# The last chunk of an expert layer finished as two half chunks, in two PSUM banks and with two stores

## The reference, cut to what matters

```python
g = jnp.einsum('th,ehi->tei', x, w1)            # 16 experts, inner width 64
u = jnp.einsum('th,ehi->tei', x, w3)
act = jax.nn.silu(g) * u
expert_out = jnp.einsum('tei,eih->teh', act, w2)
out = jnp.einsum('teh,te->th', expert_out, scores)   # scores: 4 of 16 experts are non-zero
...
x = _layernorm(x + out)        # (x - mean) / sqrt(var + 1e-5), over the 128 features of a token
```

## Time and profile before

| what | value |
| --- | --- |
| median of 3 runs | 384.11 us |
| lowest, highest run | 382.1, 384.95 us |
| the profiled execution's own time | 384.47 us |
| its span, as the trace shows it | 382.7 us |
| mean granted TensorE clock in it | 0.958 of full speed |
| TensorE, VectorE, ScalarE, GpSimd busy | 89%, 71%, 58%, 57% of the span |

### The profile page before, as it was taken

One profiled execution on the slowest core, in us unless ns is written; L12 is line 12 of the kernel. 1 busy time (PEld: TensorE's weight loads), 2 busy tenths in 40 slices (PEclk: granted clock), 3 DMA queues, 4 the chain that ended last, 5 costly groups with the idle time before them and its releaser, 6 DMA issues.

```text
span 382.7 us, 11549 instructions
## 1 busy us (share of the span) xinstructions
PE 339.9 (89%) x3556; PEld 264.8 (69%) x3556; DVE 270.0 (71%) x1247; ACT 222.7 (58%) x527; POOL 217.4 (57%) x405
## 2 busy tenths in 40 slices
PE   2876899999998998987889899999989999999992
PEld 1764687877777786875768688888755766565661
DVE  5733899999999989986647567777956259444444
ACT  1446488888999986867587566765553342222120
POOL 8667354688888887687873234330115355454551
PEclk9989589999999999999699899999999999999997
DMA  6989958888888898714654746565016410533411
GB/s 127 228 207 216 195 139 208 217 184 205 184 184 172 204 212 197 136 38 98 150 133 103 150 107 144 125 149 103 2 61 200 135 55 0 131 124 120 130 27 27
DMA packets 76927, 52.89 MB, mean 138 GB/s; under 512 B 34448, under 2 KB 68064, under 8 KB 76880
## 3 DMA queue, kind: packets, MB, share of 16 engines
q1 hardware_dynamic: 75840, 51.73, 57.1%
q0 software_dynamic: 512, 0.48, 1.0%
q10 hardware_dynamic: 528, 0.10, 0.1%
HBM read 32.24 MB, written 20.05 MB: 137 GB/s over the span
## 4 chain that ended last, share of the span: by engine, by line
issue 27%; PE 27%; POOL 23%; DVE 10%; ACT 5%; DMA 4%; SPq 2%; POOLq 1%; ACTq 0%; DVEq 0%
PE bank L1047 4%; PE bank L1051 4%; POOL rest L484 4%; POOL parts L490 4%; PE bank L1060 4%; POOL rstd L531 3%; DMA stk<-parts_dram 3%; PE bank L923 3%; PE bank L680 2%; PE bank L730 1%; POOL mixc L511 1%; SPq L361 1%; POOL gained L538 1%; PE bank L787 1%; DVE bank L1480 1%
## 5 line engine op out<-in xcount | busy, mean ns | idle before, releaser
L1480 DVE CUSTOM_DVE_ANT_0 bank<-bank,decayed_e 128x128 f32<-128x128 f32 x256 | 67.0, 323 | 1.0 <-issue 0.5
L649 POOL TENSOR_TENSOR stk<-stk 128x512 f32<-128x512 f32 x32 | 40.6, 1270 | 38.5 <-ACT stk L1354 35.8
L1491 DVE TENSOR_REDUCE top<-bank 128x4 bf16<-128x512 f32 x64 | 43.9, 687 | 22.4 <-PE bank L741 22.0
L1158 ACT ACTIVATE prob_t<-bank 128x512 f32<-128x512 f32 x64 | 38.7, 605 | 31.6 <-PE bank L770 31.1
L484 POOL TENSOR_TENSOR rest<-pf,parts 128x512 f32<-128x512 f32 (+1 forms) x32 | 29.2, 914 | 38.0 <-ACT parts L1137 37.7
L1354 ACT ACTIVATE stk<-bank 128x512 f32<-128x512 f32 x32 | 19.1, 597 | 53.6 <-PE bank L1047 53.6
L1148 ACT ACTIVATE prob<-bank 128x512 f32<-128x512 f32 x64 | 39.2, 613 | 18.2 <-PE bank L720 17.6
L1734 DVE TENSOR_TENSOR stk<-bank,stk 128x512 f32<-128x512 f32 x32 | 22.0, 691 | 39.1 <-POOL stk L649 38.0
L787 PE MATMUL bank<-prob_t,vmix 128*32 128x128 f32 x1024 | 43.0, 281 | 5.9 <-ACT pvs L1182 5.9
L490 POOL TENSOR_TENSOR parts<-rest,parts 128x512 bf16<-128x512 f32 (+1 forms) x32 | 29.3, 915 | 28.9 <-ACT parts L1141 28.7
L1468 DVE TENSOR_TENSOR decayed_e<-bank,decay 128x512 f32<-128x512 f32 x64 | 43.8, 685 | 0.5 <-issue 0.3
(11 more groups left out here) (201 smaller groups left out, 801.4 us busy)
## 6 DMA issues: line engine op xcount, KB each, us to landing
stk<-parts_dram SPq DMA_DIRECT2D x32, 384.0 KB, 5.3
stk<-shares_dram SPq DMA_DIRECT2D x64, 128.0 KB, 3.1
parts_dram<-parts SPq DMA_DIRECT2D x32, 192.0 KB, 2.4
parts_dram<-parts SPq DMA_DIRECT2D x48, 128.0 KB, 2.6
stk<-parts_dram SPq DMA_DIRECT2D x32, 192.0 KB, 3.7
parts_dram<-parts SPq DMA_DIRECT2D x32, 96.0 KB, 2.0
parts_dram<-parts SPq DMA_DIRECT2D x48, 64.0 KB, 1.8
w<-in_L_ffn_w_dram SPq DMA_DIRECT2D x3, 512.0 KB, 9.3
```

What stands on the lines that cost most here:

```text
L649: pool.tensor_tensor(h1[kk % 2], sg[kk % 2], share[kk], ALU.mult).then_inc(weighted, 1)
L1480: m = dve.tensor_tensor_reduce(out=bank[g % 2][:, 128 * j:128 * j + 128], in0=bank[g % 2][:, 128 * j:128 * j + 128], in1=decayed_e[:, g % ...
L1491: dve.tensor_reduce(top[:, b.par, GH * g:GH * g + GH], bank[S2_BANK[g % 2]][:].rearrange("p (h t) -> p h t", h=GH), AX.X, ALU.max).then_in ...
```

## The change

Chunks 0 to 2 are as before. In chunk 3 the down products of token blocks 0 and 1 go to bank 5 and those of blocks 2 and 3 to bank 7, in the same order of matmuls; of the last step each pair counts a semaphore of its own. The end of chunk 3 is made of four functions on VectorE, each for one half (two blocks), called in the order sum 0, statistics 0, sum 1, mean 0, statistics 1, mean 1, rows 0, rows 1. GpSimd makes one root of two columns for each half, and SyncE one store of 128 KB for each half. Seven semaphore names, eight semaphores in all, are new. The diff, with only the declarations cut:

```diff
...
@@ sync @@
-            store(NCH - 1)
-            sp.wait_ge(stored, 16 * NCH)
+            for m in range(2):
+                at = 4 * (NCH - 1) + 2 * m
+                sp.wait_ge(half_out[m], 2)
+                sp.dma_start(out[at:at + 2].rearrange("b t d -> t b d"), fout[:, 2 * m:2 * m + 2, :]).then_inc(stored, 16)
+            sp.wait_ge(stored, 16 * (NCH + 1))
@@ gpsimd @@
-            final_root(NCH - 1)
+            for m in range(2):
+                pool.wait_ge(half_eps, m + 1)
+                pool.tensor_tensor(frstd[:, 2 * m:2 * m + 2], fveps[:, 2 * m:2 * m + 2], minus_half[:, 0:2], ALU.pow
+                                   ).then_inc(half_root, 1)
@@ tensor @@
+            def down_halves(kk):
+
+                u = (NCH - 1) * KC + kk
+                pe.wait_ge(glu, u + 1)
+                if kk == 0:
+                    pe.wait_ge(ftail, (NCH - 2) * FT - FT + 1)
+                    pe.wait_ge(route_ev, 2)
+                for m in range(2):
+                    to = bank[(5, 7)[m]]
+                    for t in range(2 * m, 2 * m + 2):
+                        i = pe.matmul(to[:, 128 * t:128 * t + 128], actt[u % 3][:, 128 * t:128 * t + 128], w2[:, kk, :],
+                                      start=(kk == 0 and t == 2 * m), stop=(kk == KC - 1), skip_group_check=True)
+                    if kk == KC - 1:
+                        i.then_inc(down_half, 1)
+                    elif m == 1:
+                        i.then_inc(down, 1)
+
@@ in chunk(c) of tensor @@
-                    if u >= 0:
+                    if u >= 0 and u // KC < NCH - 1:
                         down_product(u // KC, u % KC)
+                    elif u >= 0:
+                        down_halves(u % KC)
@@ after the chunks @@
-            down_product(NCH - 1, KC - 2)
-            down_product(NCH - 1, KC - 1)
+            down_halves(KC - 2)
+            down_halves(KC - 1)
@@ vector @@
-            finish(NCH - 1, 0)
-            finish(NCH - 1, 1)
+
+            def add_half(m):
+                at = 4 * (NCH - 1) + 2 * m
+                dve.wait_ge(down_half, m + 1)
+                dve.tensor_tensor(fres[:, 2 * m:2 * m + 2, :],
+                                  bank[(5, 7)[m]][:, 256 * m:256 * m + 256].rearrange("p (b n) -> p b n", b=2),
+                                  x2[:, at:at + 2, :], ALU.add).then_inc(half_sum, 1)
+
+            def stats_half(m):
+                dve.wait_ge(half_sum, m + 1)
+                for t in range(2 * m, 2 * m + 2):
+                    dve.bn_stats(fstats[:, t, :], fres[:, t, :]).then_inc(half_stats, 1)
+
+            def mean_half(m):
+                dve.wait_ge(half_stats, 2 * m + 2)
+                carry()
+                for t in range(2 * m, 2 * m + 2):
+                    dve.bn_aggr(fmv[:, t, :], fstats[:, t, :]).then_inc(half_mv, 1)
+                dve.wait_ge(half_mv, 2 * m + 2)
+                dve.tensor_scalar(fveps[:, 2 * m:2 * m + 2], fmv[:, 2 * m:2 * m + 2, 1], EPS, None, ALU.add
+                                  ).then_inc(half_eps, 1)
+
+            def norm_half(m):
+                dve.wait_ge(half_root, m + 1)
+                for t in range(2 * m, 2 * m + 2):
+                    dve.tensor_scalar(fout[:, t, :], fres[:, t, :], fmv[:, t, 0:1], frstd[:, t:t + 1],
+                                      ALU.subtract, ALU.mult).then_inc(half_out[m], 1)
+
+            dve.wait_ge(ftail, (NCH - 1) * FT)
+            add_half(0)
+            stats_half(0)
+            add_half(1)
+            mean_half(0)
+            stats_half(1)
+            mean_half(1)
+            dve.wait_ge(stored, 16 * (NCH - 1))
+            norm_half(0)
+            norm_half(1)
```

More of the change, by code:

```diff
@@ L308, in build @@
         frs = sem("frs")
+        down_half = sem("down_half")
+        half_sum = sem("half_sum")
+        half_stats = sem("half_stats")
+        half_mv = sem("half_mv")
+        half_eps = sem("half_eps")
+        half_root = sem("half_root")
+        half_out = [sem("half_out0"), sem("half_out1")]
         FT = 10
```

## The result

The changed kernel took 381.81 us in the median of 20 runs (378.76 to 384.88), the kernel before 383.25 in 20 runs of the same comparison (379.74 to 385.35): a ratio of 0.9951, 95% interval 0.993 to 0.9971 (the two medians alone divide to 0.9962). One run of the changed kernel, the one of 384.88, fell in a slower state of the chip and isn't in the ratio. That is 0.5% faster, inside the range and inside the 1% band of the prediction, and it is clear of no change, which the prediction had held a measurement hardly able to show. The profiled execution took 382.46 us.

What follows compares the result with a forecast made beforehand. It took the serial 7.2 us chain after the last matmul as the bound at the end; 0.45 - 0.04 + 0.51 + 0.50 gave 1.42 us, so 384.11 less 1.4 is 382.7 us, range 381.4 to 384.6.

Steps and rivals of the forecast that it cites:

- the 1% band of the prediction: Whole measured time: a difference within 1% (3.8 us) of the kernel before, given 0.93; faster 0.04, slower 0.03.
- Early release: Last down product: its first half is ready early, so VectorE's first sum starts 0.45 us earlier.
- Sums: VectorE's two 256-column half sums: 0.42 us each by interpolation, bounds 0.34 and 0.69.
- Roots: GpSimd's two-column roots: 0.70 us each, between 0.549 for one column and 1.010 for four.
- Rival 1: GpSimd roots: each costs 1.01 us whatever its width, 0.43 lost, gain 1.0, 383.1 us; chance 0.12.
- The chain between: First sum to last root: statistics, means, epsilons and roots in halves, losing 0.04 us up to the root.
- Port: First half's rows on VectorE beside GpSimd's second root: interference taken as 0, at worst 0.26 us.
- Landing: Last store, 128 KB: 1.82 us from issue to landing instead of 2.32, 0.50 saved; bounds 1.6 and 2.3.
- Sum: End of chunk 3: 0.45 release, less 0.04, plus 0.51 fewer rows, plus 0.50 smaller store: 1.42 us earlier.

Runs made afterwards that it cites:

- late_release: Changed kernel, but both half sums wait until the whole last down product is done; tail (last down product's start to span's end) 7.45 us against 7.0.
- one_wait: Changed kernel plus a 0.06 us memset between the wait for ftail and the first sum, so the sum waits for one semaphore; tail 6.93 us.
- wide_pool: Changed kernel plus a 128 x 512 GpSimd multiply behind the second root, its result unread; tail 7.94 us, 0.93 more.
- one_store: Changed kernel with one 256 KB store behind the last row instead of two of 128 KB; tail 7.53 us, 0.52 more.
- after_again: The changed kernel itself timed once more against the kernel before (the second comparison): 382.17 us against 382.99, ratio 0.9985; tail 7.00 us.
- three_edits: Changed kernel with last half stored from two queues, GpSimd adding the first epsilon, and a memset before the first sum; 381.52 us, ratio 0.9949 against before.
- one_root: Changed kernel with one GpSimd root of four columns behind the second epsilon instead of two of two; tail 7.99 us, 0.98 more.

## Which step of the prediction failed, and what was right

The mechanism held, and every term of the sum was hit to 0.07 us. What failed is the step from the gain to what a measurement would say, in the prediction's words "A difference of 1% (3.8 us) is about what a measurement of this kernel can tell from none". That term was mis-sized. It was taken from three runs that spread over 2.85 us; in the comparison of 20 runs each the 95% interval is 0.2% wide to either side, some 0.8 us, and the kernel moved by 0.49%, beyond it. So the forecast of a gain that would hardly be told from no change was wrong: the first comparison told it. The second (ratio 0.996 to 1.001) did not, and both agree with a true 0.36%, the tail's 1.38 us.

The level failed with it. 384.11 was the median of three runs; with 20 runs the kernel before has 383.25, so the whole forecast, 382.7 for a measured 381.81, stood 0.9 too high, more than half of the gain. The prediction took the scatter into its range but kept the level, and didn't ask where the scatter comes from. That the two medians of the first comparison differ by 1.44, so near to 1.4, is luck: the ratio of the same runs makes it 1.9, and the medians of the second comparison 0.8. What can be compared with the forecast to 0.1 us is the tail. Its terms, one by one:

1. *Early release*: 0.45 of release came, and late_release shows all of it at the end. What was off is the part beside it, "VectorE starts 0.04 later, as it does now": it starts 0.11 later, since the first sum has a second wait, and the one that ends last was made an instruction of its own. That is the whole miss of the sum's start, 0.82 for 0.75 after the product's start, and one_wait gives it back.
2. *Sums*: 0.43 and 0.41, for 0.42 interpolated.
3. *Roots*: 0.70, for 0.70 interpolated between one and four columns. Rival 1 falls on its first number.
4. *The chain between*: root 1 ends 4.11 after the product's start, for 4.09: most of the 0.07 late start was won back in one place. Statistics 1 were issued 0.08 after epsilon 0's start, where 0.11 had been taken from rows 6 (another pair of instructions); the rest is in steps of 0.01 or less. From the first sum's start to root 1's end it is 3.30 us in both kernels, so the halves lost nothing there where 0.04 was counted. Rows 0 began 0.09 later than forecast, 3.35 after the product's start for 3.25, again behind a wait of its own (L1835); root 1 ended later still, so that cost nothing.
5. *Port*: taken at 0, and 0 it was. One row of the trace with the same operation (a root beside a two-input VectorE instruction) outweighed both the rule of the Trainium skill and the chunk 2 row of a wider instruction. wide_pool shows that the choice of instruction matters: a 128 x 512 multiply beside rows 1 costs 0.93, two thirds of the gain. It wasn't put beside rows 0.
6. *Landing*: 1.84 for 1.82, and 0.48 less than before where 0.50 was counted; one_store shows it.
7. *Sum*: 1.38 for 1.42. The first sum starts 0.38 earlier (0.45 counted), 0.01 is won up to root 1's end (0.04 lost), 0.51 from there to the last store's issue (0.51) and 0.48 in the landing (0.50). The experiments that take one part back cost 0.45 (release), 0.52 (store), 0.60 (rows beside the root); two of them also have a small gap of their own, so they need not add up to 1.38.

## What to carry to other kernels

Halving a serial end pays where the chain runs over several engines: the gain is the earlier release, plus the part of each last link that shrinks with its width (two rows, half the packets), and the time in which one half's rows hide beside the other's root. Put it together from per-column prices, which interpolate well between two widths (0.42 and 0.70 here, both hit to 0.01). Give an instruction on such a chain one wait only, and let an idle instruction carry waits that are already met; where it must have two, look in the trace which of them became an instruction of its own. Ask what GpSimd runs beside VectorE's rows before you overlap them. When the gain is smaller than the scatter, compare the trace from a common event onward, not the whole times; and don't take what a comparison of 20 runs can tell from the spread of three.

## What the runs showed of the hardware that was not expected

- In the 13 profiled executions all scatter sits ahead of the experts' first VectorE product: it starts between 288.1 and 293.7 us, and from there to the last one it is 81.4 us in each. The granted clock of TensorE was 1.00 from 292 to 373 us in both kernels, and 0.95 (before) and 0.96 (changed) in the stretch ahead. In the 20 runs of the changed kernel the span goes with the mean granted clock: 377.0 us at 0.979, 383.1 at 0.960 (correlation -0.75; -0.70 and -0.66 in the 12 runs each of after_again and three_edits, only -0.41 in the 23 of the kernel before). That the clock is the cause is not shown.
- A wait that stands in the queue as an instruction of its own costs 0.07 us when it is the one that ends last, on VectorE (first sum, first row, where an instruction had two waits) and on GpSimd (the root of one_root) alike; on VectorE it is 0.02 us long and the next instruction starts 0.05 after it. On SyncE, ahead of one_store's store, it cost 0.04. Where an instruction had two waits, the one written last in the program was it, in all four places named under one_wait.
- A root on GpSimd, 0.70 us long, and two VectorE rows from SBUF to SBUF run beside each other at full pace, while beside a 128 x 512 multiply on GpSimd two such rows take 1.53 instead of 0.60.
